# Cross-attention in a three-layer block: three weighings joined to a block's first scores, rows of scores spread wider, VectorE's order made anew, partition quarters by one-element maxima

## What is computed

```python
def _L0_xattn_ref(x, y, Wq, Wk, Wv, Wp, bp):
    q = _split_heads(x @ Wq)
    k = _split_heads(y @ Wk)
    v = _split_heads(y @ Wv)
    attn = jnp.einsum('bhid,bhjd->bhij', q, k) * SCALE
    attn = jax.nn.softmax(attn, axis=-1)
    out = jnp.einsum('bhij,bhjd->bhid', attn, v)
    ...
    return out @ Wp + bp
```

## Time and profile before

| | |
|---|---|
| time, median of 3 runs | 1810.27 us (1810.23 to 1812.09) |
| the profiled execution: its own time | 1810.56 us |
| its span | 1808.8 us |
| TensorE matmul (PE) busy | 1791.4 us, 99% |
| TensorE weight loads (PEld) busy | 1557.7 us, 86% |
| VectorE (DVE) busy | 1306.2 us, 72% |
| ScalarE (ACT) busy | 827.4 us, 46% |
| GpSimd (POOL) busy | 898.4 us, 50% |

### The profile page before, as it was taken

The page is one execution under the profiler, slowest core; times in us unless marked ns, Lnnn a source line. Parts: engine busy times, 40 slices in busy tenths (PEclk is TensorE's granted clock), DMA queues, the critical chain, the costliest instruction groups (busy, mean ns, idle before and its releaser), DMA issues. The chain is left out here.

```text
span 1808.8 us, 65801 instructions
## 1 busy us (share of the span) xinstructions
PE 1791.4 (99%) x28780; PEld 1557.7 (86%) x28780; DVE 1306.2 (72%) x1942; ACT 827.4 (46%) x982; POOL 898.4 (50%) x824
## 2 busy tenths in 40 slices
PE   8999999999999999999999999999999999999998
PEld 7979898989898989898989888888888887778887
DVE  6865959595969686877778686869696967574265
ACT  4634545454545454444445444545453524344232
POOL 0343737373737373737364646465555654344111
PEclk9999999999999999999999999999999999999999
DMA  6210202020202020202020201111020232123110
GB/s 254 112 54 3 84 3 83 4 83 3 84 3 83 4 83 3 83 3 84 3 83 9 78 21 66 42 45 65 22 83 3 76 114 69 26 91 107 37 59 24
DMA packets 43359, 101.20 MB, mean 56 GB/s; under 512 B 19120, under 2 KB 20656, under 8 KB 42960
## 3 DMA queue, kind: packets, MB, share of 16 engines
q1 hardware_dynamic: 43088, 96.88, 15.2%
HBM read 86.48 MB, written 8.29 MB: 52 GB/s over the span
## 5 line engine op out<-in xcount | busy, mean ns | idle before, releaser
L556 POOL TENSOR_TENSOR fold<-fold,prob 128x256 f32<-128x256 f32 x698 | 705.9, 1011 | 55.2
L114 PE MATMUL ring<-y_parts,w_keep 128*128 128x402 f32 (+1 forms) x3072 | 607.7, 351 | 1.5 <-PEq L192 1.4
L114 PEld LDWEIGHTS ring<-y_parts,w_keep 128*128 128x128 f32 x3072 | 551.4, 188 | 16.2 <-issue 3.1
L114 PE MATMUL ring<-wv_s,y_parts 128*128 128x512 f32 x2304 | 545.1, 395 | 0.0
L114 PEld LDWEIGHTS ring<-wv_s,y_parts 128*128 128x128 f32 x2304 | 430.7, 188 | 98.7
L550 POOL TENSOR_TENSOR fold<-prob 128x256 f32<-128x256 f32 x64 | 80.4, 1256 | 623.4 <-ACT prob L610 623.4
L579 ACT ACTIVATE k_sb<-ring 128x402 f32<-128x402 f32 (+1 forms) x256 | 129.4, 506 | 362.3 <-PE ring L114 362.3
L770 DVE TENSOR_TENSOR prob<-prob,peak_rows 128x1024 f32<-128x1024 f32 (+1 forms) x192 | 261.7, 1416 | 1.6
L604 ACT ACTIVATE prob<-s_ps 128x1536 f32<-128x1536 f32 (+1 forms) x128 | 200.0, 1562 | 127.8 <-PE s_ps L919 127.8
L735 DVE TENSOR_TENSOR fold<-fold,prob 128x512 f32<-128x512 f32 x192 | 173.0, 901 | 79.6 <-ACT prob L604 73.9
L610 ACT ACTIVATE prob<-prob 128x1024 f32<-128x1024 f32 (+1 forms) x192 | 210.9, 1125 | 7.4 <-DVE prob L770 5.1
(11 more groups left out here) (214 smaller groups left out, 1622.2 us busy)
## 6 DMA issues: line engine op xcount, KB each, us to landing
y_raw<-yT SPq DMA_DIRECT2D x48, 804.0 KB, 7.1
y_raw<-yT SPq DMA_DIRECT2D x16, 792.0 KB, 9.9
f_raw<-w_ffn SPq DMA_DIRECT2D x22, 512.0 KB, 3.6
v_sb<-y_left SPq DMA_DIRECT2D x1, 2304.0 KB, 11.3
v_sb<-v_left SPq DMA_DIRECT2D x16, 130.0 KB
p_x<-x SPq DMA_DIRECT2D x4, 512.0 KB, 6.5
q_scratch<-p_x SPq DMA_DIRECT2D x8, 256.0 KB, 2.1
q_sb<-q_scratch SPq DMA_DIRECT2D x16, 128.0 KB, 9.2
```

The costliest lines, as they stand in the source:

```text
L114: mm = pe.matmul(out, left(a, c), right(b, c), start=(c == 0 and n == 0), stop=(c == DC - 1 and n == 2))
L556: pool.tensor_tensor(acc[0:m], acc[0:m], prob[0:m, i, t, :], ALU.add).then_inc(sum_step, 1)
```

## The change

TensorE's list in the steady loop becomes

```diff
-        WARM = 48
+        WARM = 56
```

ScalarE, `keys_phase`:

```diff
-                for i in range(1, NBLK):
-                    key(b, i, 0)
-                    score(b, i - 1, 0)
-                    key(b, i, 1)
-                    score(b, i - 1, 1)
...
+                key(b, 1, 0)
+                score(b, 0, 0)
+                key(b, 1, 1)
+                key(b, 1, 2)
+                score(b, 0, 1)
+                key(b, 1, 3)
...
+                key(b, 2, 0)
+                key(b, 2, 1)
+                score(b, 1, 0)
+                exponential(b, 0, 0)
+                exponential(b, 0, 1)
+                key(b, 2, 2)
+                exponential(b, 0, 2)
+                key(b, 2, 3)
+                score(b, 1, 1)
+                key(b, 3, 0)
+                key(b, 3, 1)
+                key(b, 3, 2)
+                score(b, 2, 0)
+                key(b, 3, 3)
+                exponential(b, 1, 0)
+                exponential(b, 1, 1)
+                exponential(b, 1, 2)
```

ScalarE, `values_phase`:

```diff
+                score(b, 2, 1)
+                value(b, 1)
                 score(b, 3, 0)
-                value(b, 1)
-                score(b, 3, 1)
+                value(b, 3)
                 exponential(b, 2, 0)
                 exponential(b, 2, 1)
+                score(b, 3, 1)
                 exponential(b, 2, 2)
-                value(b, 3)
+                value(b, 5)
```

VectorE, `row_of_peaks`:

```diff
                 for k, rows in others:
-                    dve.tensor_copy(quarters[first, k, :], quarters[rows, 0, :]).then_inc(row_step, 1)
+                    dve.tensor_reduce(quarters[first, k, :], quarters[rows, 0, :].unsqueeze(2), AX.X,
+                                      ALU.max).then_inc(row_step, 1)
...
                 for k, rows in others:
-                    dve.tensor_copy(peak[rows, :], peak[first, :]).then_inc(row_step, 1)
+                    dve.tensor_reduce(peak[rows, :], peak[first, :].unsqueeze(2), AX.X,
+                                      ALU.max).then_inc(row_step, 1)
```

VectorE, `keys_phase` and `values_phase`:

```diff
                 largest(b, 0, 0)
+                if past:
+                    output(b - 1, 1)
                 largest(b, 0, 1)
-                for i in (1, 2):
-                    if past:
-                        output(b - 1, i)
-                    row_of_peaks(b, i - 1)
-                    subtract(b, i - 1)
-                    largest(b, i, 0)
...
-                    largest(b, i, 1)
+                row_of_peaks(b, 0)
+                subtract(b, 0)
                 if past:
-                    output(b - 1, 3)
+                    output(b - 1, 2)
+                largest(b, 1, 0)
...
+                largest(b, 1, 1)
+                row_of_peaks(b, 1)
+                subtract(b, 1)
...
                 value(b, 0)
+                if past:
+                    output(b - 1, 3)
+
+            def values_phase(b, more):
+                largest(b, 2, 0)
+                largest(b, 2, 1)
+                value(b, 2)
                 row_of_peaks(b, 2)
                 subtract(b, 2)
-
-            def values_phase(b, more):
-                value(b, 2)
+                value(b, 4)
                 largest(b, 3, 0)
                 largest(b, 3, 1)
-                value(b, 4)
+                value(b, 6)
                 row_of_peaks(b, 3)
-                value(b, 6)
                 subtract(b, 3)
                 value(b, 8)
                 if more:
```

TensorE, `batch` (the rest is the two lists above):

```diff
+            def weigh_next(b, i):
+                small_read(b, i - 1)
+                weigh(b, i)
...
+                keys(b, 1, 0)
+                scores(b, 0, 0)
+                if past and not last:
+                    weigh_next(b - 1, 1)
+                keys(b, 1, 1)
+                if last:
+                    weigh_next(b - 1, 1)
+                keys(b, 1, 2)
+                scores(b, 0, 1)
```

More of the change, by code:

```diff
@@ L630, in keys_phase @@
                     value_weights()
[L631 to L645 removed]
+                key(b, 1, 0)
[4 more added lines that the diff above has]
+                key(b, 1, 3)
+                if not past:
+                    for j in range(LEFT_SLOTS):
+                        left_high(j)
+                key(b, 2, 0)
[15 more added lines that the diff above has]
+                exponential(b, 1, 2)
                 if not past:
@@ L949, in weigh, with batch @@
                 mm.then_inc(pv_ok, 1)
-            def batch(b, past):
-                for i in range(NBLK):
-                    keys(b, i, 0)
-                    if i:
-                        scores(b, i - 1, 0)
-                    keys(b, i, 1)
-                    if i:
-                        scores(b, i - 1, 1)
-                        keys(b, i, 2)
-                    if past:
-                        small_read(b - 1, i - 1)
-                        weigh(b - 1, i)
-                    if i == 0:
-                        keys(b, i, 2)
-                    keys(b, i, 3)
+            def weigh_next(b, i):
+                small_read(b, i - 1)
+                weigh(b, i)
+            def batch(b, past, last=False):
+                keys(b, 0, 0)
+                keys(b, 0, 1)
+                if past:
+                    weigh_next(b - 1, 0)
+                keys(b, 0, 2)
+                keys(b, 0, 3)
+                keys(b, 1, 0)
[7 more added lines that the diff above has]
+                scores(b, 0, 1)
+                keys(b, 1, 3)
+                keys(b, 2, 0)
+                keys(b, 2, 1)
+                scores(b, 1, 0)
+                if past and not last:
+                    weigh_next(b - 1, 2)
+                keys(b, 2, 2)
+                if last:
+                    weigh_next(b - 1, 2)
+                keys(b, 2, 3)
+                scores(b, 1, 1)
+                keys(b, 3, 0)
+                keys(b, 3, 1)
+                keys(b, 3, 2)
+                scores(b, 2, 0)
+                if past and not last:
+                    weigh_next(b - 1, 3)
+                keys(b, 3, 3)
+                if last:
+                    weigh_next(b - 1, 3)
                 if not past:
@@ L975, in batch @@
                 values(b, 1)
+                values(b, 2)
+                scores(b, 3, 0)
+                values(b, 3)
+                values(b, 4)
                 scores(b, 3, 1)
-                for t in range(2, VT):
+                for t in range(5, VT):
                     values(b, t)
```

17 lines of the change are left out of this document (8 added, 9 removed).

## The result

The changed kernel takes 1821.79 us (median of 6 runs, 1820.67 to 1822.36), beside 1810.38 us before (6 runs): a ratio of 1.0061, with an interval of 1.005 to 1.0071. It is slower by 11.4 us. The profiled execution has a span of 1820.3 us for 1808.8.

| stretch | before, us | after, us | difference |
|---|---|---|---|
| start to K00 of batch 0 | 38.52 | 38.06 | -0.46 |
| batch 0 | 105.12 | 105.14 | +0.02 |
| 14 loop batches | 1233.30 (88.09 each) | 1241.75 (88.70 each) | +8.45 |
| last batch | 88.11 | 89.13 | +1.02 |
| all that follows | 343.71 | 346.17 | +2.46 |

What follows compares the result with a forecast made beforehand. TensorE bounds the kernel before, with VectorE only 1.9 us ahead; after the change VectorE's chain bounds the loop. 10.5 (loop) + 0.9 (last batch) = 11.4 on 1810.56 gives 1822.0, less 0.3 for the median: 1821.7 us, range 1801 to 1831.

Steps and rivals of the forecast that it cites:

- TensorE's own part: TensorE's list in a loop batch: three joins save 0.2 us each (bounds 0 and 0.5), 87.4 instead of 88.05.
- V0 ends at 52.4, and its copy starts VectorE's run: In a loop batch V0 ends 52.4 us in, before 54.6; its copy releases VectorE at 52.5, after 1.4 us lost.
- VectorE's chain of 36.2 us: VectorE from V0's copy through V10's: 37.0 - 2.0 + 0.5 = 35.5 us, with V10's copy 36.2.
- the first term: Quarters of blocks 2 and 3 on VectorE: twelve one-element maxima take 2.4 us for copies' 4.43, 2.0 less.
- TensorE waits 1.3 us, 88.8 a batch, +10.5 in the loop: At each loop batch's head TensorE waits for V10's copy: 88.8 us for 88.05, +0.75 times 14.
- V8's copy is met just so: In a loop batch V8's copy ends at 84.0 us, and V11, which needs it, starts at 84.6.
- The last batch, +0.9: V8's copy ends 3.9 us later; the low part had been 3.0 us ahead of the output product: +0.9.
- SyncE's loads keep their order: SyncE's loads stay in order; the next queries' load starts 8 us later, with some 30 us until S00; no cost added.
- WARM at 0: At the opening, eight more transposes cost 0, covered by 0.56 us idle behind them; 0.7 us at most otherwise.
- TensorE never waits: Rival, chance 0.2: VectorE's chain takes 34.9 us, only 0.6 us a batch saved on TensorE remain, 1801.9 us.
- the joins don't save anything: Rival, chance 0.12: a weighing behind scores costs what it cost behind keys; batch 89.4, +19.8 us, 1830.
- the two cancel: Rival, chance 0.13: a chain of 35.2 to 35.7 us gives batches of 87.8 to 88.3, 1807 to 1814 us.

Runs made afterwards that it cites:

- e8: The kernel of e1 with VectorE's copy of value tile 8 moved ahead of the subtraction of block 3: 1803.32 us, loop batch 87.44.
- e5: The changed kernel without joins in the loop, each weighing by itself behind a key product: 1826.74 us, loop batch 89.03.
- e6: The changed kernel with block 2's first maxima ahead of V0's copy on VectorE: 1815.49 us, loop batch 88.38.
- e2: The changed kernel with the copies of before in place of one-element maxima: 1833.99 us, loop batch 89.50.
- e1: The changed kernel with the second low part moved behind VectorE's copy of value tile 10: 1811.72 us, loop batch 88.01.
- e11: The changed kernel with the load of the queries' last rows put behind the last weighing: 1827.82 us.
- e13: The kernel of e8 with e6's early maxima and, in the last batch, the output weights' low part ahead of block 3's partition step: 1802.36 us.
- e7: The kernel before with 56 opening transposes for 48 (WARM = 56): 1810.76 us.
- e9: The kernel before with only W1 and W2 joined to S00 and S10 in the loop batches: 1810.85 us, loop batch 87.95.
- e3: The kernel before with its three weighings W1, W2 and W3 joined to scores in the loop batches, nothing else: 1814.93 us.
- e10: The kernel of e6 with S21 ahead of V0 again, on TensorE and in ScalarE's list: 1805.77 us, loop batch 87.61.

## Why the prediction was right, and where it was not

The time came out at 1821.79 for 1821.7, but two errors cancelled in it. Step by step:

- **TensorE's own part.** Right. Predicted 87.4 a batch, measured 87.44 without waits (e8); 0.2 a join, measured 0.21 (e5), so the 0.5 is excluded. The rule of the Trainium skill ("TensorEngine Tiling (Array Packing)", Key Properties), by which the joined pair keeps one drain, would give the same; no row shows the drain itself.
- **V0 ends at 52.4, and its copy starts VectorE's run.** Right as a time: the copy started at 52.58. Incomplete as a cause: S21's exponentials come 0.3 us behind it (e6). The step counted S21's move for V0's end alone and not for who waits for S21.
- **VectorE's chain of 36.2 us.** Measured 36.07. Row by row its terms come close: the twelve operations between quarters of blocks 2 and 3 take 2.07 us for 4.43 (-2.4, for -2.0), and block 2's first two maxima 2.27 for 1.98 (+0.3, for +0.5). The subtractions of both blocks, which had no term, take 8.00 for 7.62 (+0.4). But the cause given for the first term was wrong by more than half. Taking the maxima back costs only 0.8 (e2): the new order had by itself moved block 2's partition step into a pause of GpSimd's, where copies take 1.09 for 2.25, and with maxima block 3's subtraction falls beside GpSimd. I had taken both to run as they had before, so that the term came out is in part luck.
- **TensorE waits 1.3 us, 88.8 a batch, +10.5 in the loop.** The mechanism was right, the size off by a fifth: 1.03 us, 88.70, +8.45. Of the 2.05 too much 1.4 come from the batch, and 0.6 from the base, since the batch I had read took 88.05 and the mean was 88.09. Against e8's 87.44 the wait costs a batch 1.26 us, more than the idle time of 1.03 that it shows, where the prediction had 1.4.
- **V8's copy is met just so.** True for V11's products, which didn't wait. But TensorE's queue did, and the page at the loop's jump with it. It cost nothing here, as V10's copy was later still. It was to cost 8 us (14 times 88.01 - 87.44) as soon as the chain was cured: that is what e1 ran into.
- **The last batch, +0.9.** Right: +1.02. The low part ended 3.9 us later in the batch than before (89.02 for 85.10 us), as predicted.
- **"SyncE's loads keep their order", costed at nothing.** Wrong: +2.46 us, the size of what the loop had too little, so that the sum fell on the measured time by luck. They kept their order but not their times. The first of them waits for a low part that comes 3 us later, and the three then hold up TensorE's instructions (e11, e13).
- **WARM at 0.** Right (e7). The 0.46 us at the opening are scatter: K00 of batch 0 lay between 37.99 and 38.52 us in all other profiled executions of both WARM values, but for e9's 40.66.

So +8.45 + 1.02 + 2.46 - 0.46 + 0.02 = 11.49 us on the span, against a predicted 11.4 from 10.5 and 0.9 alone.

Of the rivals, "TensorE never waits" described what e8 then showed to be possible (1803.3 measured, 1801.9 worked out); "the joins don't save anything" fell with e5; "the two cancel" needed a chain of 35.2 to 35.7 us and fell with its 36.07.

## What to carry to other kernels

When a term of a sum rests on a neighbour's activity (a copy that is slow beside GpSimd), look up in the new order whether the neighbour is active at the new place, and what a shorter instruction pushes beside it; a duration doesn't move with its instruction. When an engine's list is through earlier or later, ask three times who waits: for its result, for the bank it frees (the queue behind that wait holds jumps and instruction pages too), and for the transfer that its result lets go. And a gain behind the present bound has to be tested with that bound removed: one change of place gave 10 us and a second one 8 us more, though I would expect nothing of the second alone (no run has it alone), since V10's copy would still have been later.

## What the runs showed of the hardware

- Queue 8, "instruction", moves packets of 16 KB (256 in each execution, 4.19 MB, for all engines), and most of them follow TensorE's list in pace. Where TensorE stood still, it went on 1.2 to 1.8 us after such a packet had landed (e3, e1). The Trainium skill ("Runtime: NRT & Kernel Launch", Instruction fetch mechanics) describes blocks of 16 KiB, a stall at a taken branch, and otherwise a fetch that is mostly hidden. The size and the branch agree with e1. That it is otherwise hidden doesn't hold here: a small product and its weight load go by in 14 ns (208 in 2.9 us), and such a row stood still in mid-loop for up to 1.1 us (e3), and for 1.26 us in e10.
- An instruction packet came 2.6 us late behind three loads of about 1 MB each, and TensorE stood still for 1.52 us; with the third load moved away it did not (e11).
- A copy of 32x8 elements on VectorE took 0.16 us with GpSimd still. Beside it three took 1.00 to 1.18 together, but not evenly: one that started inside an addition of GpSimd's lasted until 0.02 to 0.03 us after that addition's end. That is so for 156 of the 171 that started inside one in the kernel before; the other 15 started with 0.1 us or less of it left and took 0.16. Here the addition ends at 818.24 and the copy at 818.26:

```profile
817.50 0.74 POOL L556 TENSOR_TENSOR fold<-fold,prob 128x256 f32<-128x256 f32 x1
817.56 0.70 DVE L756 COPY quarters<-quarters 32x8 f32<-32x8 f32 x1
```

  A one-element maximum of the same size took 0.15 us in both cases (86 started inside an addition in the changed kernel). Here the copy's price was what was left of the neighbour's instruction.
